# Splitting the normalised attention output on GpSimd and turning it with 16-bit matmuls

## The reference, cut to what matters

```
q = prelu(w1 . gn(x) + b1)          # 24 x 4096 of each image
k = prelu(w2 . gn(x) + b2)          # 24 x 4096
v = prelu(wa . gn(x) + ba)          # 192 x 4096
out[n, :] = sum_m softmax_m(q[:, n] . k[:, m]) v[:, m]
x2 = x + out transposed to channels x positions
y  = x2 + likelihood(gn(x2))        # a small four-layer network for each channel
```

## Time and profile before

| | |
|---|---|
| median of 3 runs | 4913.06 us (4908.9 to 4914.46) |
| the profiled execution's own time | 4902.9 us |
| its span, first to last instruction | 4901.1 us |
| granted TensorE clock, mean | 0.983 |
| busy: PE / DVE / ACT / POOL | 91% / 84% / 76% / 15% |

### The profile page before, as it was taken

The page is one execution under the profiler, slowest core; times in us unless marked ns, Lnnn a source line. Parts: engine busy times, 40 slices in busy tenths (PEclk is TensorE's granted clock), DMA queues, the critical chain, the costliest instruction groups (busy, mean ns, idle before and its releaser), DMA issues.

```text
span 4901.1 us, 106397 instructions
## 1 busy us (share of the span) xinstructions
PE 4448.2 (91%) x38328; PEld 2967.5 (61%) x38328; DVE 4138.8 (84%) x5433; ACT 3730.4 (76%) x4214; POOL 742.2 (15%) x825
## 2 busy tenths in 40 slices
PE   6999889998899989999899998999989998899976
PEld 4887338873488725886258862688616885178821
DVE  6897898978999789996899968999698986989866
ACT  2776887769877697776977769777697776977787
POOL 4200300003010130001200022000220103101012
PEclk9999999999999999999999999999999999999988
DMA  3001431014301152011521024210341113420133
GB/s 79 14 17 32 109 84 30 23 43 114 79 23 32 36 124 68 23 32 46 122 59 31 23 63 116 48 34 21 72 111 47 31 30 74 104 51 23 34 88 94
DMA packets 154988, 279.93 MB, mean 57 GB/s; under 512 B 37441, under 2 KB 37921, under 8 KB 152706
## 3 DMA queue, kind: packets, MB, share of 16 engines
q1 hardware_dynamic: 154434, 272.69, 22.5%
HBM read 205.24 MB, written 50.33 MB: 52 GB/s over the span
## 4 chain that ended last, share of the span: by engine, by line
PE 56%; DVE 15%; ACT 13%; issue 12%; DMA 2%; SPq 1%; POOL 0%; DVEq 0%; ACTq 0%; POOLq 0%
PE ps L1407 11%; PE ps L1409 11%; PE ps L1411 10%; PE ps L1183 7%; PE ps L1359 6%; ACT th L710 6%; DVE mxp L1095 5%; ACT arena L703 4%; DVE arena L991 3%; DVE th L1029 3%; PE ps L1280 2%; PE ps L1266 2%; PE ps L1238 2%; PE ps L1227 2%; DMA arena<-x2d 1%
## 5 line engine op out<-in xcount | busy, mean ns | idle before, releaser
L1407 PE MATMUL ps<-v_sb,arena 128*128 128x193 f16 x8192 | 2015.7, 246 | 14.6 <-DVE arena L991 14.6
L1409 PE MATMUL ps<-v_sb,arena 128*128 128x192 f16 x8192 | 2024.6, 247 | 0.0
L1411 PE MATMUL ps<-v_sb,arena 128*128 128x193 f16 x8192 | 2007.5, 245 | 0.0
L667 ACT ACTIVATE arena<-ps 128x1024 f16<-128x1024 f32 x1024 | 1049.2, 1025 | 762.5 <-PE ps L1183 757.6
L991 DVE TENSOR_TENSOR arena<-arena 128x1024 f16<-128x1024 f32 x1024 | 1295.3, 1266 | 252.8 <-ACT arena L670 252.7
L1095 DVE TENSOR_REDUCE mxp<-ps 128x1 f32<-128x512 f32 x1792 | 1178.1, 686 | 50.2 <-PE ps L1359 40.0
L1029 DVE SCALAR_TENSOR_TENSOR th<-th,gates,ps 128x1024 f32<-128x1024 f32 x768 | 950.5, 1276 | 206.4 <-ACT th L710 201.5
L670 ACT ACTIVATE arena<-ps 128x1024 f32<-128x1024 f32 x1024 | 1046.3, 1022 | 0.2 <-DVE arena L991 0.2
L1409 PEld LDWEIGHTS ps<-v_sb,arena 128*128 128x128 f16 x8192 | 793.9, 97 | 262.7 <-issue 0.3
L710 ACT ACTIVATE th<-ps,biases 128x1024 f32<-128x1024 f32 x768 | 825.9, 1116 | 115.7 <-PE ps L1266 80.0
L1407 PEld LDWEIGHTS ps<-v_sb,arena 128*128 128x128 f16 x8192 | 791.2, 97 | 143.6 <-issue 26.5
(11 more groups left out here) (129 smaller groups left out, 3266.2 us busy)
## 6 DMA issues: line engine op xcount, KB each, us to landing
x<-x2d SPq DMA_DIRECT2D x1152, 64.0 KB, 2.4
arena<-x2d SPq DMA_DIRECT2D x768, 64.0 KB, 2.6
xp<-x_dram SPq DMA_DIRECT2D x18, 1536.0 KB, 12.8
shared<-x_dram SPq DMA_DIRECT2D x64, 384.0 KB, 3.7
x2d<-shared SPq DMA_DIRECT2D x64, 384.0 KB, 3.0
res<-x2d SPq DMA_DIRECT2D x96, 256.0 KB
out_dram<-res SPq DMA_DIRECT2D x96, 256.0 KB
kst<-shared SPq DMA_DIRECT2D x32, 256.0 KB, 4.5
```

Source lines behind the costliest of these rows:

```text
L667: act.activation(e_hi[:, q % 4, :].rearrange("p (k n) -> p k n", k=2), sc, ACT.Exp)
L1407: pe.matmul(acc, eh, v_sb[:, m, 0:C + 1], start=(m == 0 and t % 2 == 0), stop=False, skip_group_check=True)
L1409: pe.matmul(acc[:, 0:C], eh, v_sb[:, m, VW:VW + C], start=False, stop=False, skip_group_check=True)
L1411: ins = pe.matmul(acc, el, v_sb[:, m, 0:C + 1], start=False, stop=(m == MT - 1), skip_group_check=True)
```

## The change

For every block but the last, `o_sb` is split by POOL into a 16-bit high part and a 16-bit remainder (`o_parts`, new, 128 x 2 x 768 f16), each in one instruction over all 768 columns. PE turns the parts with plain matmuls against the 16-bit identity `eye16`, the two parts summed in PSUM: eight matmuls of 128 columns for each half where four f32 transposes stood. The last block of each image keeps `turn_out`. The POOL loop of `phase_b` now runs over the 8 blocks: in iteration j >= 1 it first splits the output of block j - 1 and only then runs `sums` and `difference` of the unit of iteration j.

```
+        o_parts = sb("o_parts", [P, 2, NT, C], F16)
...
+            def split_out(b, j):
+                normalised = pool.compute_val(b * BLOCKS + j + 1 + START)
+                turned = pool.compute_val(b * 2 * BLOCKS + 2 * j + START)
+                cast = pool.compute_val(b * (BLOCKS - 1) + j + 1)
+                settle(pool)
+                pool.wait_ge(out_norm, normalised)
+                pool.wait_ge(out_turn, turned)
+                pool.tensor_copy(o_parts[:, 0, :, :], o_sb[:, :, :]).then_inc(out_hi, 1)
+                pool.wait_ge(out_hi, cast)
+                pool.tensor_tensor(o_parts[:, 1, :, :], o_sb[:, :, :], o_parts[:, 0, :, :], ALU.subtract
+                                   ).then_inc(out_split, 1)
...
             def phase_b(b, l):
-                for u in range(UNITS - LATER, UNITS):
-                    if u == UNITS - LATER + 4:
+                for j in range(BLOCKS):
+                    if j == 4:
                         moments(b, 0)
-                    if l is not None:
-                        sums(l, u)
-                        difference(l, u)
-                moments(b, 1)
+                    if j == BLOCKS - 1:
+                        moments(b, 1)
+                    if j >= 1:
+                        split_out(b, j - 1)
+                    if l is not None and j < LATER:
+                        sums(l, UNITS - LATER + j)
+                        difference(l, UNITS - LATER + j)
                 root1(pool.compute_val(b + 1))
...
+            def turn_parts(j, h):
+                for t in range(NT):
+                    for k in range(2):
+                        ins = pe.matmul(ps[0:HALF, out_bank(j, h), t * P:(t + 1) * P],
+                                        o_parts[:, k, t, h * HALF:(h + 1) * HALF], eye16[:, :], start=(k == 0),
+                                        stop=(k == 1))
+                ins.then_inc(out_turn, 1)
...
                             if p == 12:
-                                pe.wait_ge(out_norm, blocks + START)
+                                pe.wait_ge(out_split, b * (BLOCKS - 1) + j)
                             elif not last:
                                 pe.wait_ge(max_rows, blocks + 2)
-                            turn_out(j - 1, p - 12)
+                            turn_parts(j - 1, p - 12)
```

More of the change, by code:

```diff
@@ L268, in program @@
         out_norm = sem("out_norm")
+        out_hi = sem("out_hi")
+        out_split = sem("out_split")
         out_turn = sem("out_turn")
```

## The result

| | before | changed |
|---|---|---|
| median, 18 runs each | 4909.73 us | 4918.26 us |
| lowest and highest | 4902.0, 4920.94 | 4911.31, 4924.86 |
| profiled execution, span | 4902.9, 4901.1 | 4922.7, 4920.9 |
| granted clock, mean, of the profiled execution | 0.983 | 0.976 |

A forecast was written before the change was run, and what follows sets the result against it. PE and DVE were taken as both full in attention pairs 0 to 10, PE alone in the last five. Terms +2 - 11 + 2.4 + 2, say -4.5 us, gave a median of 4908.6 us, range 4899 to 4934.

The forecast's parts named there:

- The bound and the slack: Attention pairs 0 to 10: PE and DVE both full; DVE absorbs 0.15 to 0.18 us of delay, PE loses the rest.
- The turns: PE, pairs 12 and 13: eight 16-bit matmuls cost +0.015 to +0.02 us a turn over four f32 transposes, +2 us in all.
- Rival B: PE's turns: 16-bit matmuls paced at 0.080 to 0.083 us each, +23 to +26 us in place of +2; chance 0.10.
- The second stall: Pair 6 of blocks 1, 2 and 4, seven images: L991 no longer held by POOL's `sums`, 21 x 0.53 = -11 us.
- The split: POOL at the block's start: cast 0.81 us, subtraction 1.59 to 1.78, delaying L991; 0.05 us a block, +2.4 us.
- In the last block: Last block of each image: POOL's subtraction meets DVE's third L991 and PE waits, some 0.25 x 8 = +2 us.
- `sums` stayed behind DVE: Block's start: `sums` follows the split when L991 has already taken its turn, and ends before the next; costs nothing.
- rival C: Block's start: `sums` gets ahead of the second pair's L991 at the SBUF port, +39 us, 4945; chance 0.05.
- A to E: Five rivals: no new stall 0.15, slower matmul pacing 0.10, POOL ahead at port 0.05, longer subtraction 0.10, second stall moved 0.05.

The follow-up runs named there:

- e3: Kernel before, with each of POOL's three instructions of a unit made to wait until an L991 has ended (pairs 6, 7 and 8): 4870.31 us, ratio 0.9917.
- e2: Kernel before with POOL's new order alone (`sums` of the next unit after the block's output is normalised), no split, f32 turns: 4899.43 us, ratio 0.9975.
- e1: Changed kernel with the turns as four f32 transposes again, the split still made but not read: 4906.85 us, ratio 1.000.
- e18: Kernel of e3 with 56 small matmuls of 8 columns ahead of the turn in block 1 of each image: 4916.19 us, ratio 1.0008.
- e17: Kernel of e1 with 56 small matmuls of 8 columns ahead of the turn in block 1 of each image: 4940.47 us, ratio 1.0062.

## Why the prediction was wrong, point by point

**The bound and the slack: right.** Any delay of an L991 beyond 0.15 to 0.18 us is lost on PE, and e3 shows the whole of it, 33.7 us in the blocks where its expectation had 36.

**The turns: right.** +0.01 to +0.02 us each; 0.44 for eight against 0.43 to 0.44 for four. f32 transposes were already at half the 16-bit rate, so there was nothing to win on PE. Rival B (0.080 to 0.083 each) falls, and with it, for this chip and shape, the Trainium skill's figure of about 81 ns for a stream of loads and matmuls of 128 columns (TensorE: Matmul & The Clock Gate, "Back-to-back issue gap"): measured 55.

**The second stall: right.** -11 us was the forecast; e2 has -10.7 in its blocks and -9.4 (+-1.9) in all.

**The split: right, a little dearer.** Cast 0.82 (0.81), subtraction 1.64 (1.59 to 1.78), L1010 late by 0.24, 0.08 us a block against the 0.05 taken. In the last block +0.4 us an image in the mean against 0.25. Together some 7 against 4.4 (the blocks of e1, which has the split and the old turns, are 6.9 us longer than those of e2). `sums` stayed behind DVE, as the rows said; rival C did not come. The blocks' sum is -2.7 against -4.5, and that difference is these sizes.

**What failed is the step that isn't written there:** the sum has terms for the attention blocks alone, and takes the rest of the image as it was. I priced the added PE instructions by their time in pairs 12 and 13, and let the second-layer phase, whose instructions the change doesn't touch, stand. That term, put at nothing without a reason, measured +10.8 us (+13.8 in the repetition), against -2.7 in the blocks. The experiments tie it to the number of PE instructions in the loop, with two kernels that fit badly; how they bring it stays open but for some 1.3 us at the turn-back. None of the rivals had it: A to E are all in the blocks. The range held the median, but the sign was wrong, and what the measurement can tell (1.0009 to 1.0024) is on the slow side.

## What to carry to other kernels

Where VectorE is full and has an instruction with two SBUF inputs in its rhythm, place GpSimd's instructions between two of those by a wait on VectorE's own count: here three waits a unit gave 0.8%, with no other change. Before replacing a transpose by plain 16-bit matmuls, read the spacing of the f32 ones; at 0.108 us for 128 columns two 16-bit passes buy nothing. And judge a change with a repeated measurement of the whole, not of the stage: with the blocks known to 0.1 us the other 46% of the time moved by more than the change itself.

## What of the hardware I had not expected

- With 28 to 168 short matmuls added to a loop's body of 4790, the time outside the place where they stand was longer by some 10 us (+2.8 to +13.8), and not in proportion to their number; where four or eight wide matmuls made a round longer by 0.9 or 1.7 us, it stayed within 3 us of before.
- At each turn-back of the loop PE's first matmul came 1.62 to 2.12 us after the end of a 16 KB packet of kind "instruction" (120 cases, correlation 0.98), and 0.2 us later in the changed kernel than before.
- An f32 transpose of 128 columns takes 0.108 us, and eight 16-bit matmuls that do the work of four take the same 0.44 us, though each has its own load of 96 columns.
- 56 matmuls of 8 columns in a row within an otherwise full stretch went with a granted clock of 0.97 over their block in three images of eight (e18) and four of eight (e17), and with 1.00 in the others. Such a block lasted 1.65 us longer (51.57 against 49.92, e18).
